# A graph layer's edge scan on one core: merged exponentials, products and row copies

## The reference

```
xn  = layernorm(x)
x   = x + GNN(xn, src, dst) + MIX(xn)      # GNN: 4 heads of 64, 100000 edges; MIX: linear attention, 8 heads of 32
x   = x + FFN(layernorm(x), edge_index)    # a small graph attention (4 heads of 4, 131072 edges) routes 4 experts
```

```
e   = leaky_relu(e_src[src] + e_dst[dst])
m   = segment_max(e, dst);  ex = exp(e - m[dst]);  den = segment_sum(ex, dst)
out = segment_sum(ex / den[dst] * z[src], dst)
```

## Time and profile before

| | us |
|---|---|
| timed runs (3) | median 3594.51, 3592.44 to 3606.05 |
| span of the profiled execution | 3619.3 |
| first edge loop (GNN), about 483 to 1650 | 1167 |
| carry and nodes, about 1650 to 1860 | 210 |
| second edge loop with the experts, about 1860 to 3450 | 1590 |
| TensorE (PE) busy | 1464.3, 40% |
| VectorE (DVE) busy | 1738.3, 48% |
| ScalarE (ACT) busy | 1386.9, 38% |
| GpSimd (POOL) busy | 2173.4, 60% |

### The profile page before, as it was taken

The page is one execution under the profiler, slowest core; times in us unless marked ns, Lnnn a source line. Parts: engine busy times, 40 slices in busy tenths (PEclk is TensorE's granted clock), DMA queues, the critical chain, the costliest instruction groups (busy, mean ns, idle before and its releaser), DMA issues. The chain is left out here.

```text
span 3619.3 us, 23786 instructions
## 1 busy us (share of the span) xinstructions
PE 1464.3 (40%) x4490; PEld 918.6 (25%) x4490; DVE 1738.3 (48%) x3400; ACT 1386.9 (38%) x3540; POOL 2173.4 (60%) x2136
## 2 busy tenths in 40 slices
PE   2556610211212112211514665656665656663014
PEld 1333410111111111111512333433343333332003
DVE  7667786877778777864922111111111111111137
ACT  1332346666776677752402222322222222221112
POOL 0543656666666666645666666666666666666750
PEclk8677855555555555555556777867787777776557
DMA  3421645565666656636521111111111111111166
GB/s 127 130 63 53 170 130 178 199 197 183 199 199 207 192 184 203 196 113 197 149 86 17 33 36 33 38 21 36 36 36 35 33 24 36 35 35 36 17 203 234
DMA packets 227607, 391.61 MB, mean 108 GB/s; under 512 B 53316, under 2 KB 184051, under 8 KB 220113
## 3 DMA queue, kind: packets, MB, share of 16 engines
q1 hardware_dynamic: 137556, 258.07, 20.5%
q0 software_dynamic: 80880, 124.27, 14.9%
q10 hardware_dynamic: 9100, 8.50, 0.7%
HBM read 201.15 MB, written 189.55 MB: 108 GB/s over the span
## 5 line engine op out<-in xcount | busy, mean ns | idle before, releaser
L1229 POOL DMA_INDIRECT stage_got<-ffn_rows,stage_idx x1024 | 1033.8, 1010 | 546.1 <-issue 326.6
L1229 POOL DMA_INDIRECT edges_got<-gnn_rows,edges_idx x728 | 727.9, 1000 | 354.3 <-issue 310.6
L1340 DVE TENSOR_TENSOR_SCAN stage_y<-stage_decays,stage_y 128x960 f32<-128x960 f32 (+2 forms) x288 | 527.1, 1878 | 172.8 <-ACT stage_y L1348 94.9
L2151 PE MATMUL stage_ph<-ffn_xt_all,stage_w 128*128 (+1 forms) x896 | 428.4, 618 | 284.0 <-ACT stage_hid L2205 78.7
L1363 ACT ACTIVATE stage_rows<-stage_y 128x896 f32<-128x896 f32 x224 | 372.5, 1816 | 7.7 <-issue 7.7
L2233 DVE TENSOR_TENSOR search_found<-stage_po,stage_b 128x256 f32<-128x256 f32 x196 | 75.9, 420 | 579.8 <-DMA x_again_X<-in_x_dram 425.3
L1637 PE MATMUL stage_pm<-setup_ident,stage_mix_parts 128*128 128x128 f32 x98 | 32.4, 434 | 778.7 <-ACT stage_mix_parts L1663 634.5
L1327 ACT ACTIVATE stage_y<-edges_got,stage_y 128x64 f32<-128x64 f32 x784 | 230.9, 393 | 244.2 <-issue 200.9
L2163 PE MATMUL stage_po<-stage_w,stage_start_parts 128*128 128x256 f32 x784 | 243.6, 437 | 189.9 <-issue 153.6
L2151 PEld LDWEIGHTS stage_ph<-ffn_xt_all,stage_w 128*128 128x128 f32 x896 | 190.6, 218 | 468.9 <-issue 372.6
L2163 PE MATMUL stage_po<-stage_w,stage_hid 128*128 128x256 f32 x784 | 237.6, 426 | 164.7 <-issue 162.4
(11 more groups left out here) (473 smaller groups left out, 2871.8 us busy)
## 6 DMA issues: line engine op xcount, KB each, us to landing
state_gnn<-stage_rows SPq DMA_DIRECT2D x56, 1848.0 KB
y<-search_found SPq DMA_DIRECT2D x28, 896.0 KB
tail_fin_y<-y SPq DMA_DIRECT2D x7, 3584.0 KB
stage_got<-ffn_rows,stage_idx POOLq DMA_INDIRECT x1024
edges_got<-gnn_rows,edges_idx POOLq DMA_INDIRECT x784
state_ffn<-stage_rows SPq DMA_DIRECT2D x64, 192.0 KB
mix_rows<-stage_mix_parts SPq DMA_DIRECT2D x49, 131.0 KB
x_again_mix<-mix_rows SPq DMA_DIRECT2D x7, 917.0 KB
```

Source lines behind the costliest of these rows:

```text
L1229: pool.indirect_dma_start(out=got[:, u, t, :], out_offset=None, in_=self.row_dram[g.name][:, :], in_offset=bass.IndirectOffsetOnAxis(ap=id ...
L1340: ins = dve.tensor_tensor_scan(some, r[s][:, 0:b - a, :].rearrange("p c t -> p (c t)"), some, 0.0, ALU.mult, ALU.add)
L2151: mm = pe.matmul(ph[:, n % 4, 0:HALF], w1[:, e, k, f * P:(f + 1) * P], xt_all[:, k, bass.ds(b * (B * P) + half * HALF, HALF)], start=(k == ...
```

## The change

- `act_exps`: the exponential into `w` is gone. The weights are read from where the denominators' own exponential stands, in `y`. The decays of all four heads are one instruction instead of four.
- `dve_weigh`: `w` is now that part of `y`, in SBUF. For FFN one product covers the four heads. The wait for `rows_ready` is left to ScalarE, ahead of the exponential.
- `act_rows`: the rows are stored in the scan's own column order (q, h, k), with one copy in place of five for GNN. FFN's is as it was.
- What reads states takes the new order: the last states in `dve_end` (one copy less), the products and the table in `carry`, with the `affine_select` once a pass, and the division in `nodes_and_rows`, one product a pass in place of one.

```diff
             def act_exps(act, c, u):
                 s = u % 2
                 act.wait_ge(logits_ready, c + 1)
-                act.activation(w[:, :, :], pm[:, :, :], ACT.Exp).then_inc(w_ready, 1)
                 if not below(c, 2):
                     act.wait_ge(rows_ready, c - 1)
-                act.activation(y[:, s, C:C + H, 1:T + 1], pm[:, :, :], ACT.Exp)
-                for h in range(H):
-                    act.activation(r[s][:, h * KQ:(h + 1) * KQ, :], dl[:, h, :].unsqueeze(1).to_broadcast([P, KQ, T + 1]), ACT.Exp)
+                act.activation(y[:, s, C:C + H, 1:T + 1], pm[:, :, :], ACT.Exp).then_inc(w_ready, 1)
+                act.activation(r[s][:, 0:RC, :].rearrange("p (h k) t -> p h k t", k=KQ), dl[:, :, :].unsqueeze(2).to_broadcast([P, H, KQ, T + 1]), ACT.Exp)
                 act.activation(r[s][:, RC:RC + H, :], dl[:, :, :], ACT.Exp).then_inc(r_ready, 1)
...
             def dve_weigh(dve, c, u):
                 s = u % 2
-                if not below(c, 2):
-                    dve.wait_ge(rows_ready, c - 1)
+                w = y[:, s, C:C + H, 1:T + 1]
                 dve.wait_ge(w_ready, c + 1)
-                for h in range(H - 1 if g is GNN else H):
+                if g is FFN:
+                    dve.tensor_tensor(y[:, s, 0:C, 1:T + 1].rearrange("p (h k) t -> p t h k", h=H),
+                                      got[:, u, :, 0:C].rearrange("p t (h k) -> p t h k", h=H),
+                                      w.rearrange("p h t -> p t h").unsqueeze(3).to_broadcast([P, T, H, K]), ALU.mult).then_inc(weighed, 1)
+                    dve.drain()
+                    return
+                for h in range(H - 1):
...
-                if Q == 1:
-                    act.activation(rows[:, s, :, 0:C + H].rearrange("p t c -> p c t"), y[:, s, :, 1:T + 1], ACT.Copy).then_inc(rows_ready, 1)
-                    return
-                act.activation(rows[:, s, :, C:C + H].rearrange("p t h -> p h t"), y[:, s, C:C + H, 1:T + 1], ACT.Copy)
-                out = rows[:, s, :, 0:C].rearrange("p t (h q k) -> p q h k t", q=Q, k=KQ)
-                for q in range(Q):
-                    of_pass = y[:, s, q * RC:(q + 1) * RC, 1:T + 1].rearrange("p (h k) t -> p h k t", h=H)
-                    ins = act.activation(out[:, q, :, :, :], of_pass, ACT.Copy)
-                ins.then_inc(rows_ready, 1)
+                act.activation(rows[:, s, :, 0:C + H].rearrange("p t c -> p c t"), y[:, s, :, 1:T + 1], ACT.Copy).then_inc(rows_ready, 1)
...
-                pool.affine_select(out=spread_w[:, 0:C], in_=spread_w[:, 0:C], compare_op=ALU.is_ge, fill=0.0,
-                                   base=0, pattern=[[1, C]], channel_multiplier=-K)
+                for q in range(Q):
+                    of_pass = spread_w[:, q * H * KQ:(q + 1) * H * KQ]
+                    pool.affine_select(out=of_pass, in_=of_pass, compare_op=ALU.is_ge, fill=0.0,
+                                       base=0, pattern=[[1, H * KQ]], channel_multiplier=-KQ)
...
-                    dve.tensor_tensor(by_head(ya[:, :, :]), by_head(st[:, s, :, 0:C]),
-                                      den[:, :, :].unsqueeze(3).to_broadcast([P, G, H, K]), ALU.mult).then_inc(taken, 1)
+                    for n in range(Q):
+                        ins = dve.tensor_tensor(ya[:, :, :].rearrange("p g (h q k) -> p q g h k", q=Q, k=KQ)[:, n, :, :, :],
+                                                st[:, s, :, n * H * KQ:(n + 1) * H * KQ].rearrange("p g (h k) -> p g h k", k=KQ),
+                                                den[:, :, :].unsqueeze(3).to_broadcast([P, G, H, KQ]), ALU.mult)
+                    ins.then_inc(taken, 1)
```

More of the change, by code:

```diff
@@ L1187, in chunk_parts @@
             r = [decays[:, s, 0:(RC + H) * (T + 1)].rearrange("p (c t) -> p c t", t=T + 1) for s in range(2)]
-            w = self.ps(stack, "weights", [P, 512])[:, 0:H * T].rearrange("p (h t) -> p h t", t=T)
         else:
-            (w,) = self.several(stack, "weights", [P, H, T])
             decays = self.sb(stack, "decays", [P, 2, RC + H, T + 1])
@@ L1414, in _ @@
                 pool.drain()
-                pool.affine_select(out=spread_w[:, 0:C], in_=spread_w[:, 0:C], compare_op=ALU.is_ge, fill=0.0,
-                                   base=0, pattern=[[1, C]], channel_multiplier=-K)
+                for q in range(Q):
+                    of_pass = spread_w[:, q * H * KQ:(q + 1) * H * KQ]
+                    pool.affine_select(out=of_pass, in_=of_pass, compare_op=ALU.is_ge, fill=0.0,
+                                       base=0, pattern=[[1, H * KQ]], channel_multiplier=-KQ)
                 pool.drain()
-                pool.affine_select(out=spread_w[:, 0:C], in_=spread_w[:, 0:C], compare_op=ALU.is_gt, fill=0.0,
-                                   base=K, pattern=[[-1, C]], channel_multiplier=K)
+                for q in range(Q):
+                    of_pass = spread_w[:, q * H * KQ:(q + 1) * H * KQ]
+                    pool.affine_select(out=of_pass, in_=of_pass, compare_op=ALU.is_gt, fill=0.0,
+                                       base=KQ, pattern=[[-1, H * KQ]], channel_multiplier=KQ)
                 pool.affine_select(out=spread_w[:, C:C + H], in_=spread_w[:, C:C + H], compare_op=ALU.is_equal, fill=0.0,
@@ L1463, in _, with by_head, over_state @@
             def _(dve):
+                def by_head(ap):
+                    return ap.rearrange("p (q h k) -> p q h k", h=H, k=KQ)
+                def over_state(ap):
+                    return ap.unsqueeze(1).unsqueeze(3).to_broadcast([P, Q, H, KQ])
                 dve.memset(ends[:, :], 0.0).then_inc(ends_clear, 1)
@@ L1507, in _ @@
                 for n, state in enumerate((ends, table)):
-                    by_head = state[:, 0:C].rearrange("p (h k) -> p h k", k=K)
-                    dve.tensor_tensor(by_head, by_head, heads(parts[:, n, :], K), ALU.mult)
+                    dve.tensor_tensor(by_head(state[:, 0:C]), by_head(state[:, 0:C]), over_state(parts[:, n, :]), ALU.mult)
                     dve.tensor_tensor(state[:, C:C + H], state[:, C:C + H], parts[:, n, :], ALU.mult)
```

16 lines of the change are left out of this document (4 added, 12 removed).

## The result

The changed kernel takes 3537.4 us (median of 4 runs, 3531.6 to 3549.1) against 3593.5 for the kernel before: ratio 0.984 [0.982, 0.986]. A second measurement on another occasion gave 3542.7 us in 5 runs, ratio 0.985 [0.982, 0.988]. So the change is worth 54 to 58 us. I forecast 24 (3570 us): right in sign, less than half in size.

The account below looks back on a forecast made before the run. It took ScalarE with its slow stretch to set the first loop, the experts' products the second. First loop -22, second -4, additions +2 make -24 us: 3594.5 - 24 = 3570 us, range 3530 to 3655.

Parts of the forecast that it names:

- ScalarE's savings: First loop, ScalarE: exponential removed 0.13, decays merged 0.23, rows copied at once 0.18; 0.54 us saved a chunk.
- The weights' new place: First loop: VectorE's weighings read both inputs from SBUF, delaying GpSimd's gathers; 1.4 us lost a chunk, 2.8 a pair.
- the lock: First loop: a gather wanting to begin waits for VectorE's running two-SBUF-input product to end; 1.4 us lost a chunk.
- GpSimd's pair of 39.7 us: First loop: GpSimd's time for two chunks after the change, 36.4 + 0.5 + 2.8 us, nearly using up its slack.
- The slow stretch I leave as it is: First loop, once a pair: ScalarE's 14 weighings come 1.4 us apart instead of running through in 3.50; assumed unchanged.
- 0.8 us saved in each of 28 pairs: First loop: each two-chunk pair falls from 40.87 to 40.1 us, 22 us in all.
- Second loop, 4 us: Second loop: savings hidden under the experts' products except 0.15 us of TensorE's Gelu wait, x 28; bounds 0 and 22.
- What is added, 2 us: Node stage products +1.5 us, carry's longer affine_select lists +0.5, less two copies at loop ends; together +2 us.
- A: First loop: ScalarE's slow stretch lengthens by what the other work saves; 3592 us, chance 0.25.
- B: First loop: VectorE's products keep GpSimd's gathers out for their whole length; 3720 us, cheap end 3600 and up; chance 0.12.
- C: First loop: fewer ScalarE instructions shorten its slow stretch, leaving GpSimd's 39.7 us a pair as floor; 3540 us, chance 0.15.
- D: First loop: the long rows copy runs at 2.2 ns an element, costing 1.5 us more; 3655 us, chance 0.08.

## Why the prediction was wrong

*ScalarE's savings* (0.54 us a chunk): nearly right, 0.42. The undisturbed chunk fell from 14.35 to 13.9 us. The exponential brought 0.13 as priced, the decays 0.27 for 0.23, the rows 0.02 instead of 0.18 us.

*The weights' new place*: the size of the lock was right (1.2 us lost a chunk, forecast 1.4) and GpSimd's pair of 39.7 us nearly: where GpSimd sets the loop, in chunks 10 to 18, the pair is 39.0 to 39.6. The conclusion was wrong in sign. I booked the edit as a cost to be set against ScalarE's saving. By itself it makes the kernel 14 to 33 us faster, and no slow stretch comes in the first 14 chunks.

*"The slow stretch I leave as it is: no row tells me its cause"*, and with it *0.8 us saved in each of 28 pairs*: **this is the step that failed in the first loop.** I took the steady pair and spread a saving over 28 of them. In the steady part no saving is seen: seven profiles with the old or the new first loop put the later 41 chunks at 838 to 867 us, 20.4 to 21.1 a chunk, and the variants with more, less or moved work at 835 to 863 (two apart: the one with the drain, and the one with the read alone, 884, whose profile is of its longest execution). All of the gain, 39 us for my 22, sits in the first 14 chunks, which I had not looked at separately, although they cost 275 us in the trace of before, with five held chunks in them. There the work saved makes 0.45 x 14 = 6 us, and the rest is the slow stretch, which went from five held chunks to none (43.6 us of idle time ahead of the weighings to nothing).

*Second loop, 4 us*: **mis-sized, measured 17 (9 to 25).** I took 0.15 of TensorE's wait of 0.40 us a pair. The upper bound of 22 was near. The term took it that a saving reaches the time only through this wait; ScalarE's shorter edge work explains some 6 us by the traces, and no run shows where the others come from. TensorE's idle time as a whole did not fall (575 and 594 us before, 589 and 573 after).

*What is added, 2 us*: right as far as it can be seen. The four products of a group cost what was forecast (15.6 us busy for 14.2), and the stretch between the loops is 2.9 us longer. Kernels with its old code took 287.2 to 290.3 us there, so this is at the limit of what a profile tells.

```profile
L2012 DVE TENSOR_TENSOR nodes_gnn_node_parts<-nodes_gnn_st,nodes_gnn_node_parts 128x448 f32<-128x448 f32 x28 | 15.6, 619 | 0.5
```

*The rivals.* A (the stretch takes the saving back) describes the later 41 chunks, which is more than I gave it. B didn't come: 1.2 us lost a chunk, 1.7 in the first 14, is below its threshold of 2.0. C came near in time (3540), but its cause isn't borne out: the stretch got rarer, yet it stayed away early in a kernel with all 33 instructions, and eight more cost in time what one longer one costs. D is refuted, 3640 elements take 6.57 us. Two sums among the rivals were off: B's 150 us give 3742 with the other terms, not 3720, and D with the dear half of B makes 0.14, not the 0.20 that I gave to slower.

**Open:** what the slow stretch is. Shown: it falls on ScalarE, VectorE and TensorE, in the changed kernel on the first two in the same loop, and not on the busiest alone (in the first loop of before VectorE is busy 656 us, ScalarE 589, and it is ScalarE that has it); it is absent where GpSimd sets the pace and the others wait for it in each chunk (0 of 56 with the drain, and chunks 10 to 14 of the changed kernel); behind chunk 14 it comes with more and with fewer instructions, without the loop, and with fewer stored bytes. Not shown: whether the read keeps it away at first by itself or by slowing GpSimd by 1.7 us a chunk, and whether the recording of the profiler has a part in the stretch, which no run tests. Where ScalarE weighs and VectorE reads from `y`, chunks 0 to 13 had no held one in six profiles of ten, and 1 to 3 in four; with PSUM 4 to 6 in all seven, the kernel with the drain apart.

## What to carry to other kernels

Cut a loop into its start and its steady part before you multiply a saving by the number of turns, and compare the parts in two profiles of each kernel. Where an engine loses time that no wait explains, work taken off it may bring nothing, and an edit without any saving may bring a lot: try the parts of a change singly and undone before giving one of them the credit. A gain of which three small instructions more undo half (13 us of work, 30 us of time) is not the sum of the instructions that were saved. And when a filler is to slow an engine by a given amount, read from the trace what it did add: four memsets of 0.28 us added 0.6 us, not 1.1.

## What was unexpected

- Two kernels that differ only in where VectorE reads its 56 weights (PSUM or SBUF) differ by 36 to 43 us in 14 chunks, in favour of the one whose gathers are slower.
- A drain on GpSimd behind 14 gathers left it idle for 7.5 us a chunk, although the gathers themselves are only 1.00 us long in the profile.
- Stages with the same code take different times in profiles of kernels that differ elsewhere: 466 to 486 us ahead of the first loop, 1505.6 to 1536.1 for the changed second loop.
